# Normed attention with projections that come out transposed: head sums and roots through small tiles of the TensorE array

## The chip, the cores and the metric

The program runs on one NeuronCore of one Trainium2 chip, in one launch. The metric is the device time of that launch in microseconds (us); the median of three runs of the kernel before is 1232.67 us (1228.65 to 1232.94). The engines are called as in the profile: PE (TensorE products), PEld (its weight loads), DVE (VectorE), ACT (ScalarE), POOL (GpSimd).

## The reference, cut to what matters

Eight layers follow one another on 32 x 64 tokens of 128 numbers; each is `x = x + layer(layernorm(x))`. The change is in the third, an attention with 16 heads of 64 in which each head of the queries and of the keys is divided by its root mean square:

```python
def rms_norm(x, w):
    var = jnp.mean(jnp.square(x), axis=-1, keepdims=True)
    return x * jax.lax.rsqrt(var + EPS) * w
qh = (q @ Wq).reshape(b, l, HEADS, HEAD_DIM).transpose(0, 2, 1, 3)
kh = (kv @ Wk).reshape(b, s, HEADS, HEAD_DIM).transpose(0, 2, 1, 3)
vh = (kv @ Wv).reshape(b, s, HEADS, HEAD_DIM).transpose(0, 2, 1, 3)
qh = rms_norm(qh, q_norm_w)
kh = rms_norm(kh, k_norm_w)
scores = jnp.einsum('bhld,bhsd->bhls', qh, kh) * (1.0 / np.sqrt(HEAD_DIM))
scores = jnp.where(mask, scores, NEG_INF)
attn = jax.nn.softmax(scores, axis=-1)
o = jnp.einsum('bhls,bhsd->bhld', attn, vh)
return o.transpose(0, 2, 1, 3).reshape(b, l, HEADS * HEAD_DIM) @ Wo
```

Everything is float32. Each of the 32 sequences attends to 64 positions of its own context.

## The kernel before, in words

The 2048 tokens are 16 tiles of 128, worked on as 8 pairs of tiles (256 tokens, four sequences). Each layer is a stage that goes over the 8 pairs; each engine has its own instruction list, written by hand, and its order is the order in the code. Engines meet at semaphores. PE writes to a ring of six PSUM banks; a `Stage` holds a list of units such as `("s00", "v")`, one per filling of a bank, with the engine that empties it ("a" ACT, "v" DVE). Unit number j may fill its bank only when unit j - 6 has been emptied (`bank_free`). So the list sets both the order of fillings and who waits for whom. Two more banks lie outside the ring, one for the result (`ybank`) and one for turning the normed tokens (`xtbank`).

The normed attention (`att1`) is software-pipelined: an opening (`pro`) projects pair 0; the body (`body`, 7 times) works on the scores of pair p and on the projections of pair p + 1; a closing (`epi`) finishes pair 7. Per step of the body:

- PE: 64 products for the scores (line 1411); the queries and keys of the next pair as 8 products of 512 columns with the tokens as weights (1424); the result of the last pair (1481); 16 transposes of the probabilities (1358); 64 products for the mix (1467); the values (1440); 32 transposes of the scaled queries and keys (1452); the turn of the normed tokens (363).
- ACT: from each bank of projections a copy (1528) and a square (1529); the exponentials (1339); copies of the turned probabilities (1365); the reciprocal roots of the head sums as exp(-0.5 ln) (1553, 1555); copies of the mix (1560) and the values (1568); half of the turned queries and keys, scaled by the gain (1576).
- DVE: the softmax (mask and copy out of the bank 1315, maximum 1320, subtraction 1322, sum 1345, reciprocal 1347, product 1349); the sums of squares over each head (1591); the ending of the last pair (1864, 321 to 333: add to the stream, mean and variance, normed tokens); the division of tokens by their roots (1601); the other half of the turned queries and keys (1611).
- POOL: copies of the next inputs (2470, 2472) and the root of the variance for the ending (352).

With the tokens on the partitions, a head's sum of squares runs along a row, and the root is one number per partition and head. The scores need the head's 64 numbers on the partitions, so that the scaled tokens are transposed afterwards. The stage after next (`plain_attention`, twice) has the same softmax but no norms: its projections come out with the head's numbers on the partitions at once (1674).

## Time and profile before

| | us |
|---|---|
| median of 3 runs (lowest, highest) | 1232.67 (1228.65, 1232.94) |
| the profiled execution, its own time | 1232.76 |
| its span, first to last instruction | 1231.0 |
| PE, DVE, ACT, POOL busy | 1027.4, 855.5, 576.6, 222.0 |
[...]

Rows of a timeline read: start, duration, engine, line of the kernel, operation, what it writes and reads, how many in the group; in brackets the engine's idle time before and who ended it. On PE one product of float32 numbers is two instructions. The duration of a PE group includes the tail in which the last product leaves the array; the next group can start inside it. Busy shares are means over all stages; what matters here is one step of one stage.

### The profile page before, as it was taken

What the parts mean: (1) busy time and instruction counts of PE and PEld (TensorE: products, weight loads), DVE (VectorE), ACT (ScalarE), POOL (GpSimd) and SP (SyncE); (2) the same over time, 40 slices, a digit from 0 to 9 for tenths busy, and PEclk for the clock granted to TensorE, in tenths of its full rate; (3) what the DMA queues carried; (4) which work ended last, traced back from release to release, by engine and by line L of the source; (5) the groups of instructions that cost most, each with busy time, mean ns of one, the idle gap of its engine ahead of it and who ended that gap; (6) DMA issues with size and microseconds to landing.
All of it is one profiled execution on the core that took longest, in us unless ns stands there. A gap on an engine that the chain in (4) does not pass through costs nothing.

```text
span 1231.0 us, 32393 instructions
## 1 busy us (share of the span) xinstructions
PE 1027.4 (83%) x11974; PEld 816.6 (66%) x11974; DVE 855.5 (69%) x1903; ACT 576.6 (47%) x1119; POOL 222.0 (18%) x243
## 2 busy tenths in 40 slices
PE   5678999969888886899899999899998673798756
PEld 5357888746556566778678877678776562467546
DVE  5565677788999996555677676687675577667455
ACT  1223344556666663343555665465655220344343
POOL 3554122100111101331100000000000122343100
PEclk9877999989999998899999999999999885699778
DMA  9200000000000000000000000000000000000001
GB/s 369 95 2 1 0 0 0 0 2 2 0 0 0 0 0 2 2 1 1 2 2 0 0 0 2 2 1 0 0 0 2 1 0 0 1 1 0 1 0 34
DMA packets 5919, 16.13 MB, mean 13 GB/s; under 512 B 729, under 2 KB 4962, under 8 KB 5218
## 3 DMA queue, kind: packets, MB, share of 16 engines
q1 hardware_dynamic: 5858, 15.29, 3.2%
q8 instruction: 42, 0.69, 0.2%
q14 instruction: 19, 0.16, 0.0%
HBM read 14.24 MB, written 1.05 MB: 12 GB/s over the span
## 4 chain that ended last, share of the span: by engine, by line
PE 40%; issue 23%; DVE 18%; DVEq 11%; POOL 3%; ACT 2%; POOLq 2%; PEldq 1%; PEld 1%; ACTq 0%
PE banks L1674 7%; PE banks L1747 4%; PE banks L1719 3%; PE banks L1136 3%; PE banks L900 3%; PE banks L1707 3%; DVEq L1346 2%; PE banks L1358 2%; PE banks L1117 1%; PE banks L1735 1%; DVE small L1591 1%; DVE xn L333 1%; POOL small L832 1%; DVEq L1012 1%; DVE xr L1011 1%
## 5 line engine op out<-in xcount | busy, mean ns | idle before, releaser
L352 POOL TENSOR_TENSOR rstd<-var,nhalf 128x2 f32<-128x2 f32 x72 | 57.3, 796 | 483.0 <-DVE var L326 483.0
L1682 ACT ACTIVATE work<-banks 128x512 f32<-128x512 f32 x128 | 74.9, 600 | 70.2 <-PE banks L1674 70.2
L1339 ACT ACTIVATE work<-work 128x1024 f32<-128x1024 f32 x64 | 67.7, 1058 | 55.6 <-DVEq L1335 32.0
L374 ACT ACTIVATE xT_all<-banks 128x256 f32 (+1 forms) x72 | 28.3, 393 | 133.5 <-PE banks L363 133.0
L1674 PE MATMUL banks<-xT_all,weights 128*128 (+1 forms) x384 | 86.2, 380 | 2.3 <-ACT work L1792 1.8
L1358 PE MATMUL banks<-ident,work 128*128 128x128 f32 x512 | 71.0, 290 | 16.2 <-DVE work L1349 11.2
L1674 PEld LDWEIGHTS banks<-xT_all,weights 128*128 128x128 f32 x384 | 71.5, 190 | 13.7 <-ACT work L1792 2.6
L929 ACT ACTIVATE work<-banks,weights 128x256 f32<-128x256 f32 x128 | 53.6, 470 | 57.5 <-PE banks L890 56.5
L1358 PEld LDWEIGHTS banks<-ident,work 128*128 128x128 f32 x512 | 62.9, 150 | 23.3 <-DVE work L1349 13.3
L1826 DVE TENSOR_TENSOR work<-banks,neg_mask 128x512 f32<-128x512 f32 x64 | 40.7, 685 | 52.2 <-PE banks L1707 50.6
L363 PE MATMUL banks<-ident,xn 128*128 128x128 f32 x144 | 33.6, 320 | 43.7 <-DVE xn L333 38.4
L1747 PEld LDWEIGHTS banks<-weights,work 128*128 128x128 f32 x512 | 58.4, 191 | 14.9 <-ACT work L1792 14.8
L900 PE MATMUL banks<-weights,work 128*128 128x128 f32 x512 | 63.1, 276 | 3.7 <-DVE work L1003 3.4
L900 PEld LDWEIGHTS banks<-weights,work 128*128 128x128 f32 x512 | 60.9, 191 | 7.9 <-ACT work L929 6.9
L1747 PE MATMUL banks<-weights,work 128*128 128x128 f32 x512 | 61.0, 277 | 3.6 <-ACT work L1792 3.6
L890 PE MATMUL banks<-xs,weights 128*128 128x256 f32 x256 | 61.8, 390 | 0.0
L1349 DVE TENSOR_TENSOR work<-work,small 128x1024 f32<-128x1024 f32 x48 | 58.8, 1225 | 3.6
L1786 ACT ACTIVATE work<-banks 128x512 f32<-128x512 f32 x64 | 34.7, 595 | 55.7 <-PE banks L1735 55.5
L1345 DVE TENSOR_REDUCE small<-work 128x16 f32<-128x1024 f32 x48 | 58.2, 1212 | 0.0
L1365 ACT ACTIVATE work<-banks 128x512 f32<-128x512 f32 x96 | 52.1, 630 | 11.7 <-PE banks L1358 11.7
L1528 ACT ACTIVATE weights<-banks 128x512 f32<-128x512 f32 x64 | 41.1, 641 | 32.2 <-PE banks L1424 32.2
L363 PEld LDWEIGHTS banks<-ident,xn 128*128 128x128 f32 x144 | 18.2, 157 | 55.6 <-DVE xn L333 41.0
(311 smaller groups left out, 2413.3 us busy)
## 6 DMA issues: line engine op xcount, KB each, us to landing
weights<-wpack SPq DMA_DIRECT2D x1, 5381.5 KB, 32.1
weights<-wpack SPq DMA_DIRECT2D x1, 2060.0 KB, 13.2
weights<-wpack SPq DMA_DIRECT2D x1, 2049.0 KB, 17.5
weights<-wpack SPq DMA_DIRECT2D x1, 1160.5 KB, 19.8
x_all<-x_in SPq DMA_DIRECT2D x2, 512.0 KB, 4.8
ctxT_all<-ctxT_in SPq DMA_DIRECT2D x1, 1024.0 KB, 7.0
out<-x_all SPq DMA_DIRECT2D x8, 128.0 KB, 1.8
rows<-rows_in SPq DMA_DIRECT2D x1, 832.0 KB
```

The costliest lines, as they stand in the source:

```text
L352: g.tensor_tensor(rstd, var, nhalf[:, 0:2], ALU.pow).then_inc(rstd_ready, 1)
L890: ins = pe.matmul(bk[:, (c % 2) * PT:(c % 2 + 1) * PT], upw[:, c, :], xs[:], start=True, stop=True)
L900: ins = pe.matmul(bk[:, (2 * u + e % 2) * D:(2 * u + e % 2 + 1) * D], hT[:, e * chunks + c, u * P:(u + 1) * P], dnw[:, e * chunks + c, :], ...
L929: ins = act.activation(hT[:, c, :], bank(s.bank(name))[:, (c % 2) * PT:(c % 2 + 1) * PT], func, bias=w(pre + "_upb")[:, c:c + 1])
L1339: act.activation(sm[:, u, :], sm[:, u, :], ACT.Exp, scale=scale).then_inc(h["exp"].sem, 1)
L1345: v.reduce_sum(rs[:, u, :], every, AX)
L1349: v.tensor_tensor(every, every, rs[:, u, :, None].to_broadcast([P, 16, S]), ALU.mult) \
L1358: ins = pe.transpose(bank(s.bank(name))[:, c * P:(c + 1) * P], sm[:, u, 512 * half + c * P:512 * half + (c + 1) * P], ident[:])
L1365: act.activation(pT[:, u, 4 * half:4 * half + 4, :].rearrange("p c t -> p (c t)"), bank(s.bank(f"p{u}{half}")), ACT.Copy).then_inc(act_emp ...
L1674: ins = pe.matmul(bank(ring.bank(f"qk{c}"))[:, j * PT:(j + 1) * PT], wt[:, 2 * (c % 4) + j, :], cols(src, p), start=True, stop=True)
L1682: act.activation(dst.rearrange("p c t -> p (c t)"), bank(ring.bank(f"qk{c}")), ACT.Copy) \
L1747: ins = pe.matmul(ybank[:, u, :], oT[:, u, c, :], wo[:, c, :], start=(c == 0), stop=(c == 7))
```

## The change

The projections of queries and keys are now computed as in the plain attention: weights stationary, tokens moving, so that the heads' numbers come out on the partitions and nothing has to be transposed. A head's sum of squares then runs over partitions, and is formed by products: `head_sum` (128 x 32, ones in two columns) against the squares, on four column tiles (128 rows x 32 columns of the array each), that write to four strips of one bank. ACT makes the reciprocal roots of the bank (128 x 256). A second group of products spreads them over the partitions again, with the gains in the weights: each uses one row tile (32 rows x 128 columns) and writes one half bank. DVE multiplies the stored heads by these eight banks, in place. The squares of four of the eight banks go from ACT to POOL (`pooled`), except in the opening. The opening is moved to the end of the stage before (`tensor_head`, `scalar_head`, `vector_head`), and `make_gains`, a few small DVE operations, into its first step. POOL copies only the context.

The units of the ring, and the core of the new code:

```diff
-        att1 = pipelined(scores4, mixing8, [(f"tok{u}{c}", "a") for u in range(2) for c in range(4)],
-                         values4 + [(f"turn{u}{c}", "av"[c % 2]) for u in range(2) for c in range(4)])
+        scaling8 = [(f"bc{c}", "v") for c in range(8)]
+        att1 = stage([])
+        att1.pro = stage([("gains", "a")] + queries8 + [("sums", "a")] + scaling8 + values4, 1, shift=2)
+        att1.body = stage(scores4 + queries8 + [("sums", "a")] + turned4 + scaling8 + mixed4 + values4, PAIRS - 1)
+        att1.epi = stage(scores4 + turned4 + mixed4, 1)
...
+            pooled = (0, 2, 4, 6)
...
+            def make_gains(v):
+
+                v.wait_ge(weights_in[group], 16)
+                v.memset(head_sum, 0.0)
+                for k in range(2):
+                    v.tensor_scalar(gains[:, k, :], ident[:], w("a1_norm")[:, k:k + 1], None, ALU.mult)
+                v.drain()
+                for m in range(4):
+                    ins = v.tensor_copy(head_sum[:, m, :, 2 * m:2 * m + 2], parity[:, None, :].to_broadcast([P, 2, 2]))
+                ins.then_inc(gains_made, 1)
...
+            def sums(pe, ring, i, p):
+                settle(pe)
+                pe.wait_ge(*ring.emptied(i, "qk7"))
+                if ring is s.body and pooled:
+                    pe.wait_ge(*pool_squared.at(p - 1, 1))
+                settle(pe)
+                pe.wait_ge(*ring.bank_free(i, "sums"))
+                bk = bank(ring.bank("sums"))
+                for m in range(4):
+                    for j in range(4):
+                        ins = pe.matmul(bk[32 * j:32 * j + 32, 0:PT], head_sum[:, m, 0, :],
+                                        squares[j // 2][:, 4 * (j % 2) + m, :], start=(m == 0), stop=(m == 3),
+                                        tile_position=(0, 32 * j))
+                ins.then_inc(banks_filled, 1)
+
+            def roots_spread(pe, ring, i, p):
+                pe.wait_ge(*roots_made.at(p, 1))
+                for m in range(4):
+                    for j in range(4):
+                        name = f"bc{4 * (m // 2) + j}"
+                        if m % 2 == 0:
+                            settle(pe)
+                            pe.wait_ge(*ring.bank_free(i, name))
+                    for j in range(4):
+                        name = f"bc{4 * (m // 2) + j}"
+                        ins = pe.matmul(bank(ring.bank(name))[:, PT * (m % 2):PT * (m % 2) + PT],
+                                        gains_spread[32 * j:32 * j + 32, P * m:P * m + P],
+                                        head_roots[32 * j:32 * j + 32, :], start=True, stop=True,
+                                        tile_position=(32 * j, 0))
+                        if m % 2:
+                            ins.then_inc(banks_filled, 1)
...
+            def tensor_head(pe):
...
+                for k in range(2):
+                    for m in range(4):
+                        ins = pe.matmul(bank(s.pro.bank("gains"))[S * k:S * k + S, P * m:P * m + P],
+                                        head_sum[:, m, :, :].rearrange("p k r -> p (k r)"), gains[:, k, :],
+                                        start=True, stop=True)
...
+                def part(ring, i, p, last=True):
+                    if ring is s.body:
+                        pe.wait_ge(*ring.emptied_before(i, "bc7"))
+                        settle(pe)
+                    scores(ring, i, 0)
+                    scores(ring, i, 1)
+                    if ring is s.body:
+                        project(pe, ring, i, p + 1)
+                    if last:
+                        result([ring.emptied_before(i, f"o{u}1") for u in range(2)] if ring is s.body else None)
+                    if ring is s.body:
+                        sums(pe, ring, i, p + 1)
+                    probs_turned(pe, ring, i, p, 0, h["prob"])
+                    probs_turned(pe, ring, i, p, 1, h["prob"])
+                    if ring is s.body:
+                        roots_spread(pe, ring, i, p + 1)
+                        settle(pe)
+                        pe.wait_ge(*ring.emptied_before(i, "v3"))
+                    mix(ring, i, 0)
+                    mix(ring, i, 1)
+                    if ring is s.body:
+                        values(pe, ring, i, p + 1)
+                    turn_normed(pe, g_of(s, p))
...
+            def projected(act, ring, i, c):
+                act.wait_ge(banks_filled, ring.filled(i, f"qk{c}"))
+                k, a = c // 4, 2 * (c % 4)
+                bk = bank(ring.bank(f"qk{c}"))
+                ins = act.activation((kT if k else qT)[:, a:a + 2, :].rearrange("p c t -> p (c t)"), bk, ACT.Copy)
+                if ring is s.pro or c not in pooled:
+                    ins = act.activation(squares[k][:, a:a + 2, :].rearrange("p c t -> p (c t)"), bk, ACT.Square)
+                ins.then_inc(act_emptied, 1)
+
+            def head_roots_made(act, ring, i):
+                act.wait_ge(banks_filled, ring.filled(i, "sums"))
+                act.activation(head_roots, bank(ring.bank("sums"))[:, 0:PT], ACT.Ln, bias=eps[:, 0:1],
+                               scale=1.0 / 64).then_inc(act_emptied, 1)
+                act.drain()
+                act.activation(head_roots, head_roots, ACT.Exp, scale=-0.5).then_inc(roots_made.sem, 1)
...
+            def scaled(v, ring, i):
+                for k in range(8):
+                    v.wait_ge(banks_filled, ring.filled(i, f"bc{k}"))
+                    v.tensor_tensor(heads_of(k), bank(ring.bank(f"bc{k}")).rearrange("p (c t) -> p c t", t=PT),
+                                    heads_of(k), ALU.mult).then_inc(dve_emptied, 1)
...
+            def pool(g, p):
+
+                for c in pooled:
+                    k, a = c // 4, 2 * (c % 4)
+                    own = (kT if k else qT)[:, a:a + 2, :]
+                    g.wait_ge(*s.body.emptied(p, f"qk{c}"))
+                    ins = g.tensor_tensor(squares[k][:, a:a + 2, :], own, own, ALU.mult)
```

ACT's order in a step is: banks 0 and 1, first exponential, banks 2 to 5, second exponential, banks 6 and 7, roots, then as before.

The opening and the first step on PE, before (the names are those of the program's tensors; `banks` is PSUM, `work` holds queries, keys and probabilities, `xs` and `cs` are the pair's inputs; the 64x64 rows are scores, then mixes):

```order
L1424 MATMUL banks<-weights,xs 128x512 x2
L1424 MATMUL banks<-weights,cs 128x512 x2
L1440 MATMUL banks<-weights,cs 128x512 x4
L1452 MATMUL banks<-ident,weights 128x128 x32
L1411 MATMUL banks<-work 64x64 x64
L1424 MATMUL banks<-weights,xs 128x512 x2
L1424 MATMUL banks<-weights,cs 128x512 x2
L1358 MATMUL banks<-ident,work 128x128 x16
L1467 MATMUL banks<-work 64x64 x64
L1440 MATMUL banks<-weights,cs 128x512 x4
L1452 MATMUL banks<-ident,weights 128x128 x32
L363 MATMUL banks<-ident,xn 128x128 x2
```

The same place of PE, now (`free` with 32x256 is `head_sum` against the squares, `small,free` the roots against the gains):

```order
L1471 MATMUL banks<-work,free 64x128 x8
L1418 MATMUL banks<-xT_all,weights 128x256 x8
L1418 MATMUL banks<-ctxT_all,weights 128x256 x8
L1432 MATMUL banks<-weights,free 32x256 x16
L1447 MATMUL banks<-small,free 128x256 x16
L1460 MATMUL banks<-weights,cs 128x512 x4
L1493 MATMUL banks<-work 64x64 x64
L1352 MATMUL banks<-ident,work 128x128 x16
L1511 MATMUL banks<-work 64x64 x64
L357 MATMUL banks<-ident,xn 128x128 x2
```

The 32 transposes behind the values are gone. The sums stand behind the projections, ahead of the transposes of the probabilities, and the spread between those and the mix.

DVE in the first step behind the second maximum of the softmax, before:

```order
L1345 TENSOR_REDUCE small<-work 128x16
L1347 RECIPROCAL small<-small 128x16
L1349 TENSOR_TENSOR work<-work,small 128x1024
L1591 TENSOR_REDUCE small<-work 128x16 x4
L1594 TENSOR_SCALAR small<-small 128x64
L1601 TENSOR_TENSOR weights<-weights,small 128x1024 x4
L1611 TENSOR_SCALAR work<-banks,weights 128x4x128 x4
```

And now:

```order
L1339 TENSOR_REDUCE small<-work 128x16
L1341 RECIPROCAL small<-small 128x16
L1343 TENSOR_TENSOR work<-work,small 128x1024
L1620 TENSOR_TENSOR work<-banks,work 128x512 x8
```

Three groups behind the softmax have become one. In the later steps the ending of the last pair stands between 1343 and 1620; before, its first part stood ahead of 1601 and its second part, which needs POOL's root, behind it.

## Rows read from the trace of the kernel before

**Rows 1.** The page: span, then busy time (share) x instructions of an engine.
```profile
span 1231.0 us, 32393 instructions
...
PE 1027.4 (83%) x11974; PEld 816.6 (66%) x11974; DVE 855.5 (69%) x1903; ACT 576.6 (47%) x1119; POOL 222.0 (18%) x243
```

**Rows 2.** Timeline of PE in the stage: start, duration, what, [idle before].
```profile
258.52 2.23 PE L1411 MATMUL banks<-work 64*64 64x64 f32 x128 [1.34 <-DVE work L1611]
...
286.44 2.48 PE L1411 MATMUL banks<-work 64*64 64x64 f32 x128 [1.01 <-DVE work L1611]
...
315.93 2.53 PE L1411 MATMUL banks<-work 64*64 64x64 f32 x128 [1.28 <-DVE work L1611]
...
325.37 3.73 PE L1481 MATMUL banks<-weights,work 128*128 128x128 f32 x32
...
339.28 1.96 PE L1452 MATMUL banks<-ident,weights 128*128 128x128 f32 x16 [0.90 <-ACT work L1568]
...
462.92 2.23 PE L1411 MATMUL banks<-work 64*64 64x64 f32 x128 [1.24 <-DVE work L1611]
```

**Rows 3.** Stretches: length, PE, PEld, DVE, ACT, POOL busy (count), clock, DMA, GB/s.
```profile
315.90:345.40 29.50, 25.44 (x362) 17.75 (x363) 26.75 (x35) 19.54 (x37) 3.78 (x3) 1.00 0.00 0
638.20:659.90 21.70, 20.95 (x358) 17.27 (x348) 15.71 (x25) 13.22 (x23) 1.10 (x2) 1.00 0.00 0
```

**Rows 4.** Timeline of DVE in the third step.
```profile
317.24 1.29 DVE L1315 TENSOR_TENSOR work<-banks,neg_len 128x512 f32<-128x512 f32 x2 [1.76 <-PE banks L1411]
...
329.23 1.23 DVE L1349 TENSOR_TENSOR work<-work,small 128x1024 f32<-128x1024 f32 x1
330.37 4.59 DVE L1591 TENSOR_REDUCE small<-work 128x16 f32<-128x1024 f32 x4
...
336.79 5.03 DVE L1601 TENSOR_TENSOR weights<-weights,small 128x1024 f32<-128x1024 f32 x4
...
342.26 2.71 DVE L1611 TENSOR_SCALAR work<-banks,weights 128x512 f32<-128x512 f32 x4
```

**Rows 5.** Timeline of the plain attention, PE and the ending on DVE.
```profile
649.96 7.07 PE L1674 MATMUL banks<-xT_all,weights 128*128 x32
...
651.60 0.42 DVE L1891 TENSOR_TENSOR xr<-banks,tok_all 128x256 f32<-128x256 f32 x1
...
653.97 0.60 DVE L333 TENSOR_SCALAR xn<-xr,mv,rstd 128x128 f32<-128x128 f32 x2 [0.82 <-POOL rstd L352]
...
656.87 1.91 PE L1358 MATMUL banks<-ident,work 128*128 128x128 f32 x16
...
664.06 3.70 PE L1719 MATMUL banks<-weights,xs 128*128 128x512 f32 x8
```

**Rows 6.** Timeline of PE where small tiles stand now.
```profile
517.53 1.15 PE L1146 MATMUL banks<-free 32*128 32x256 f32 x16
...
1091.00 1.09 PE L2172 MATMUL banks<-weights,cs 128*64 128x128 f32 x16
```

**Rows 7.** Line 2172, its weight loads: ns minimum/median/maximum, first and last start.
```profile
L2172 PEld LDWEIGHTS banks<-weights,cs x128: 132/136/231, 1065.8 to 1157.3; 128*64 128x64 f32 x128
```

**Rows 8.** Timeline of ACT: first copy, last square of the opening; an exponential.
```profile
236.93 0.60 ACT L1528 ACTIVATE weights<-banks 128x512 f32<-128x512 f32 x1 [2.36 <-PE banks L1424]
...
244.09 0.78 ACT L1529 ACTIVATE work<-banks 128x512 f32<-128x512 f32 x1
...
321.17 1.06 ACT L1339 ACTIVATE work<-work 128x1024 f32<-128x1024 f32 x1 [0.53 <-DVE work L1322]
```

**Rows 9.** Groups of POOL by shape: count | busy us, mean ns | idle before.
```profile
L790 POOL TENSOR_TENSOR work<-xT_all,qmask 128x512 f32<-128x512 f32 x8 | 8.3, 1038 | 0.9 <-issue 0.8
...
L2470 POOL COPY xs<-xT_all 128x256 f32<-128x256 f32 x10 | 4.0, 396 | 16.0 <-PEq L906 7.9 <-PEq L1722 4.2 <-PEq L1443 3.9
```

**Rows 10.** Timeline of POOL in the third step.
```profile
339.35 1.39 POOL L2472 COPY cs<-ctxT_all 128x256 f32 x1
```

**Rows 11.** A stretch of the opening, columns as in rows 3.
```profile
250.00:252.00 2.00, 0.61 (x3) 0.61 (x4) 2.00 (x3) 0.88 (x2) 0.00 (x0) 0.50 0.00 0
```

More of the change, by code:

```diff
@@ L1625, in step @@
                         end[0](v, s, p - 1)
-                    if normed and nxt:
-                        divide(p + 1)
-                    if this and last:
                         end[1](v, s, p - 1)
-                    if normed and nxt:
-                        turned(ring, i)
-                step(s.pro, 0, -1, False, True)
-                step(s.body, 0, 0, True, True, last=False)
-                with v.Fori(1, PAIRS - 1) as p:
-                    step(s.body, p, p, True, True)
-                step(s.epi, 0, PAIRS - 1, True, False)
+                    if ring is s.body:
+                        scaled(v, ring, i)
```

374 lines of the change are left out of this document (149 added, 225 removed).

## Prediction

> **What bounds the kernel now.** First the page's head: the span is 1231.0 us in the profiled execution, PE is busy for 83% and DVE for 69% of it [rows 1]. These are means over eight stages, so the stage of the change is read by itself. The next view is the timeline of PE. The scores of a pair open each step of the normed attention, at 258.52 (first step), 286.44 (second), 315.93 (third), and at 462.92 for the closing one [rows 2]. The six steps between 286.44 and 462.92 take 176.48 us, 29.4 each; the first takes 27.9.
>
> The view by stretches of one such step shows DVE busy for 26.75 of 29.5 us at a full clock, PE for 25.44. One step of the following plain attention, which has the same softmax and the same products but no norms of heads, takes 21.7 us with PE at 20.95 and DVE at 15.71 [rows 3]. So the norms cost 7.7 us a step and turn a PE-bound step into a DVE-bound one. The timeline of DVE shows it: between 317.24 and the end of L1611 at 344.97 it has no idle stretch; its one wait is 1.76 us for the first scores, and the scores had waited for DVE's last L1611 [rows 2, 4]. DVE sets the end, PE stands at its back only from the last scaled bank to the first score.
>
> **What the change takes off DVE, per step.** Four sums of squares (L1591), 4.59 us; four divisions (L1601), 5.03; four scaled copies out of the transposes (L1611), 2.71; together 12.3 us with no cover, as DVE is the bound [rows 4]. It adds eight products bank x work of 128x512. Their form is that of L1315, 1.29 us for two in a row [rows 4], so 8 x 0.65 = 5.2. DVE falls from 26.7 to about 19.6 us of work in a step.
>
> **What it does to PE, per step.** Removed: the 32 transposes of scaled queries and keys (two groups of 16, L1452, 1.96 us with its tail [rows 2]), about 3.6. Unchanged in columns: the 8 projections, formerly tokens as weights with 512 columns, now 16 products of 256 columns; 32 instructions of just this kind last 7.07 in the plain attention [rows 5]. Added: 16 products for the sums and 16 for the spread, each two instructions of 256 columns. On the whole array such an instruction costs 7.07/32 = 0.22, which would be 7.1 for each of the two groups. On tiles it is less. Rows of 32 x 128 stand in the trace: 16 instructions of 256 columns in 1.15 us, a tail of about 0.2 included, against 16 x 0.22 = 3.5: nearly four run at once. Columns of 128 x 32 do not; the nearest are 128 x 64, where 16 instructions of 128 columns last 1.09, tail of about 0.25 included, against 16 x 0.11 = 1.8 on the whole array, so two column tiles run beside each other [rows 6]. Bounds for the sums are thus 1.75 (four at once) and 7.1 (in a line), with 3.6 for two at once. I take 1.85: four row tiles reach nearly four and two column tiles nearly two. The spread is 2 x 1.15.
>
> [...]
>
> **The new step, laid out.** Zero is the start of the scores.
> PE does scores until 2.5, projections until 9.5, the result product of the last pair (L1481, 3.73 with tail [rows 2]) until 13.1. The sums wait there for the copies and squares of all eight banks. ScalarE starts one such operation each 0.48 (sixteen between 236.93 and 244.09 [rows 8]) and has 12 of them and two exponentials of 1.06 [rows 8] between: the last square ends near 12.0. GpSimd's four squares cost 1.04 each by L790 [rows 9]; the last can start at about 11.1 and end at 12.2 to 13.1. So the sums run 13.1 to 14.95, and the 16 transposes of probabilities (1.91 [rows 5]) to 16.8; DVE's probabilities were ready at 14.5, as now (329.23 + 1.23 - 315.93 [rows 2, 4]). ScalarE's logarithm and exponential of 128x256, about 0.4 each, fall under the transposes. Then it copies the turned probabilities, and the fourth bank of the spread is that of the second copy, so the spread starts at about 17.1. Its first half fills four banks at 18.2.
> DVE has meanwhile done the ending of the last pair: 14.5 plus 2.97 (from 651.60 to 654.57 in the plain attention, the root by GpSimd included [rows 5]) is 17.5. That root was hidden behind the divisions; it is bare now, but it ends before the first spread bank. DVE scales two banks until 19.6. Only then may PE fill the second half, because its last two banks are those of the first two; that half is full at 20.75. The first mix needs the bank of the fourth scaling (20.9) and the second mix that of the sixth (22.2): mixes end at 23.4, values (3.70 with tail [rows 5]) at 27.0, the turn of the normed tokens at 27.3. I take 27.5 for the step.
> So PE becomes the bound, with some 2.5 us of waits for DVE left in it between 16.8 and 20.9. The gain is 29.4 - 27.5 = 1.9, though DVE loses 7: the rest is DVE idling. Behind each added wait on PE stand the mixes and values, and nobody waits for those but ScalarE.
>
> **The other terms.** Six such steps: -11.5. First step: no result product, no ending; the sums wait for the squares and the spread for the roots, 27.5 to 28.5 against 27.9: +0.1. Opening: eight products for the gains come first (about 1.8 on PE, which can start some 0.8 sooner), so the same sixteen copies and squares of ScalarE begin 1.0 later than at 236.93 and the last ends at 245.9 [rows 8]. Then sums (247.8), roots (248.9), first half (250.1), two scalings (251.4), second half (252.5), and DVE's last scaling at 255.5; the last copy of the values ends at about 257, against scores at 258.52. [...] I take -0.5, within -2 and +1.5. Seven small DVE operations that make the gains, about 1.3 us in all, lie in the stage before, where DVE waits for PE in each pair: +0.3, at most 1.3. One copy of 128x256 per pair goes from GpSimd: nothing. The stages behind are untouched.
> Sum: -11.5 + 0.1 - 0.5 + 0.3 = -11.6. The profiled execution took 1232.76, 1.76 more than its span and 0.1 above the median of 1232.67, so the forecast is 1232.8 - 11.6 = 1221.2. A measurement of this kernel tells 0.5%, 6.2 us, from no change.
>
> **Rivals.**
> 1. Column tiles run only two at a time. The sums then take 3.6, all of it on PE's path, as roots and spread follow: +1.75 in each of eight places, +14, 1235. For it: no row shows more than two. Against it: the row tiles show that four streams can be fed. 9%.
> 2. GpSimd and DVE stop each other. A copy of 128x256 on GpSimd takes 0.396 alone and 1.39 while DVE runs L1601 [rows 9, 10]. If each of the four squares holds up one of DVE's four operations with two inputs in SBUF (L1322 and L1349, twice) for its whole 1.04, DVE's probabilities come 4.1 later. PE needs the second at about 15.9 and they are ready at 14.5, so 1.4 is absorbed and 2.7 not: seven steps give +19, 1240.5, slower than before. It decides from a mean delay above 0.9 per square. Against it: ScalarE spaces the squares out, and two of them start while DVE reads a bank or reduces. 7%. [...]
> 3. The same, mild: the last square ends 1 us after PE is ready for the sums. +1 in seven steps: 1228. 8%.
> 4. [...] 3%.
> 5. PE loses less at the banks than laid out (the second half of the spread starts closer behind the first scaling, the opening keeps its clock): steps of 26.7 and -2 in the opening give 1215. It is the low end of the forecast's own case.
>
> **How the numbers follow.** Forecast with rival 5: 73%, all of it faster by over 0.5%. Rivals 1 and 3: 17%, within 0.5%. Rivals 2 and 4: 10%, slower. The range runs from 1213 (steps of 26.5, a good opening) to 1234 (nearly the whole of rival 1), and leaves out rivals 2 and 4 and a few per cent below.
>
> **What the new profile would show.** Steps of 27.5 from scores to scores. DVE idle for about 8 of them, above all before the eight products on banks. [...] The two halves of the spread 2.5 us apart, the second released by DVE. GpSimd's squares near 1.04, and L1322 and L1349 still at 1.23; longer ones mean rival 2. PE waiting at the sums for GpSimd means rival 3. I am wrong at the root if the step is again DVE's, or if PE's wait stands anywhere but between the transposes and the mixes.

## The result, and the profile after

| | median us (lowest to highest, runs) | ratio to before, 95% interval |
|---|---|---|
| before | 1232.16 (1228.65 to 1232.94, 4) | |
| after | 1241.56 (1239.11 to 1243.94, 4) | 1.0072 [1.0047, 1.0097] |

The changed kernel is slower by 0.7%, where 1221.2 us was forecast. The profiled execution took 1239.11 us, the shortest of the four. The head of its page, as in [rows 1]:

```profile
span 1237.4 us, 33362 instructions
...
PE 1027.7 (83%) x12374; PEld 830.1 (67%) x12374; DVE 800.9 (65%) x1871; ACT 549.0 (44%) x1060; POOL 245.8 (20%) x263
```

DVE lost 54.6 us of work, as meant; PE kept its 1027. The stretch of one looped step, from scores to scores (columns as in [rows 3]):

```profile
407.45:436.67 29.22, 25.59 (x410) 19.76 (x410) 19.78 (x30) 15.72 (x29) 7.21 (x6) 1.00 0.00 0
```

DVE falls from 26.75 us to 19.78, the 19.6 of the forecast, and yet the step is 29.22 us long where it was 29.49. PE is busy for 25.59 of it, so 3.6 us of waits must stand on PE. Its timeline in this step shows where:

```profile
407.45 1.21 PE L1493 MATMUL banks<-work 64*64 64x64 f32 x64 [1.08 <-issue]
...
417.10 3.73 PE L1525 MATMUL banks<-weights,work 128*128 128x128 f32 x32
420.77 1.94 PE L1432 MATMUL banks<-weights,free 128*32 128x256 f32 x32
422.64 1.97 PE L1352 MATMUL banks<-ident,work 128*128 128x128 f32 x16
424.78 1.15 PE L1447 MATMUL banks<-small,free 32*128 32x256 f32 x16 [0.17 <-ACT work L1359]
427.28 1.15 PE L1447 MATMUL banks<-small,free 32*128 32x256 f32 x16 [1.36 <-DVE work L1620]
428.57 1.16 PE L1511 MATMUL banks<-work 64*64 64x64 f32 x64
430.04 1.16 PE L1511 MATMUL banks<-work 64*64 64x64 f32 x64 [0.31 <-DVE work L1620]
431.13 3.70 PE L1460 MATMUL banks<-weights,cs 128*128 128x512 f32 x8
435.19 0.41 PE L357 MATMUL banks<-ident,xn 128*128 128x128 f32 x2 [0.35 <-issue]
436.67 1.21 PE L1493 MATMUL banks<-work 64*64 64x64 f32 x64 [1.08 <-issue]
```

Counted from the scores: sums (L1432) at 13.3, transposes (L1352) 15.2, spread (L1447) 17.3 and 19.8, mixes (L1511) 21.1 and 22.6, values (L1460) 23.7 to 27.4. The forecast had 13.1, 14.95, 17.1, 19.65, 20.9, 22.2, 23.4 to 27.0. So 0.4 us had come together by the end of the values. The rest is in the tail: 0.35 us ahead of the turn (L357), and 1.08 between it and the next scores, both "issue", that is, nobody had to be waited for.

Not all looped steps are like this one. From scores to scores, the six intervals behind the first step are 30.71, four of 29.22 to 29.24, and 28.47 to the closing step, 176.1 us in all where before had 176.48.

The waits of PE over the six such steps, summed (us in total, times, longest):

```profile
PE banks L1447 <- DVE work L1620: 8.2, 6, 1.4
PE banks L1493 <- issue: 7.7, 12, 1.1
PE banks L357 <- issue: 2.1, 6, 0.4
PE banks L1511 <- DVE work L1620: 1.9, 6, 0.3
```

Before, the scores waited for DVE 8.7 us in all over the same stretch, in seven waits of up to 1.3 [rows 2]; now they and the turn wait 9.8 us for the issue of instructions.

The opening, PE after; before, the scores stood at 258.52 [rows 2]:

```profile
240.00 3.62 PE L1418 MATMUL banks<-ctxT_all,weights 128*128 128x256 f32 x16
245.70 1.94 PE L1432 MATMUL banks<-weights,free 128*32 128x256 f32 x32 [2.08 <-ACT weights L1563]
249.43 1.15 PE L1447 MATMUL banks<-small,free 32*128 32x256 f32 x16 [1.79 <-ACT small L1571]
251.91 2.09 PE L1447 MATMUL banks<-small,free 32*128 32x256 f32 x16 [1.33 <-DVE work L1620]
253.93 5.77 PE L1460 MATMUL banks<-weights,cs 128*128 128x512 f32 x8
260.99 1.21 PE L1493 MATMUL banks<-work 64*64 64x64 f32 x64 [1.29 <-ACT work L1576]
```

After three waits (5.2 us idle of 8.3) the second half of the spread takes 2.09 us where the first took 1.15, and the values 5.77 where a looped step has 3.70. The stretch of that second half says why: the granted clock was 0.50 of the full one; over the values it was 0.64 in the mean.

```profile
251.90:254.00 2.10, 2.09 (x17) 1.29 (x17) 1.15 (x2) 0.00 (x0) 0.00 (x0) 0.50 0.00 0
253.93:259.70 5.77, 5.77 (x12) 2.23 (x8) 2.48 (x4) 1.79 (x3) 0.00 (x0) 0.64 0.00 0
```

The kernel before has a stretch at 0.50 in its opening too, from 250 to 252 [rows 11], where PE comes back from 5.04 us of waiting:

```profile
251.39 5.78 PE L1452 MATMUL banks<-ident,weights 128*128 128x128 f32 x32 [5.04 <-DVE weights L1601]
```

The third loss lies where nothing was changed. At the border of the two plain attentions the groups of 64x64 products break off and go on later:

```profile
774.73 1.95 PE L1748 MATMUL banks<-work 64*64 64x64 f32 x104
778.29 0.58 PE L1748 MATMUL banks<-work 64*64 64x64 f32 x24 [1.61 <-issue]
...
803.15 2.50 PE L1720 MATMUL banks<-work 64*64 64x64 f32 x123 [1.36 <-ACT work L1359]
806.64 0.34 PE L1720 MATMUL banks<-work 64*64 64x64 f32 x5 [0.98 <-issue]
```

The same group in the profile of before is whole:

```profile
770.13 2.38 PE L1735 MATMUL banks<-work 64*64 64x64 f32 x128
```

A mark by which kernels can be compared place by place is the start of the turn of the normed tokens on PE (L363, L357). The table gives it for before, and for the others the difference to it (negative: earlier). It is one execution of each, and ahead of the stage, where nearly the same code has run, they already differ by over 3 us; so differences between rows say more than a row.

| place | before | after | a_nodrain | e_after_split | f_open_split | c_both | e_both_split |
|---|---|---|---|---|---|---|---|
| last turn ahead of the stage | 232.25 | -0.28 | +3.08 | +2.16 | +1.62 | +1.68 | +1.79 |
| first scores | 258.52 | +2.47 | +4.30 | +6.79 | -0.16 | -0.11 | +0.01 |
| last turn before the closing step | 461.30 | +3.11 | -2.65 | +6.32 | -8.20 | -14.95 | -15.96 |
| border of the plain attentions, start | 769.71 | +4.60 | +0.17 | +4.68 | -8.86 | -10.35 | -15.14 |
| the same, end | 819.93 | +7.78 | +2.79 | +4.87 | -9.23 | -8.02 | -15.76 |
| last turn | 1174.33 | +7.34 | +5.86 | +6.45 | -11.87 | -9.55 | -17.71 |
| looped step (the fifth interval), us | 29.49 | 29.22 | 27.55 | 29.04 | 27.52 | 26.47 | 26.47 |

The miss can be laid out for the profiled executions. That of after is 6.4 us longer than that of before (1239.11 against 1232.76), where 11.6 less was forecast: a miss of 18.0 us. The six intervals hold 11.1 of them (176.1 against 6 x 27.5), the opening 3.3 (+2.75 against -0.5), and what lies behind the closing scores 4.2 (from +2.2 there to +6.4 at the end of the span); the stages ahead give 0.6 back.

### The profile page after: what moved, and what is told of

It reads as the page before. It is cut to its first block, busy times and chain, and to the rows that moved or that the text cites. A ratio compares the mean times of both kernels' runs of the same rounds, so it can differ in the third digit from the quotient of the medians.

```text
span 1237.4 us, 33362 instructions
## 1 busy us (share of the span) xinstructions
PE 1027.7 (83%) x12374; PEld 830.1 (67%) x12374; DVE 800.9 (65%) x1871; ACT 549.0 (44%) x1060; POOL 245.8 (20%) x263
## 4 chain that ended last, share of the span: by engine, by line
PE 49%; issue 21%; DVE 12%; DVEq 8%; POOL 4%; ACT 3%; POOLq 1%; PEldq 1%; PEld 0%; ACTq 0%
PE banks L1687 7%; PE banks L1760 4%; PE banks L1732 4%; PE banks L1418 3%; PE banks L1131 3%; PE banks L894 3%; PE banks L1720 3%; PE banks L1352 2%; PE banks L1460 2%; PE banks L1748 2%; PE banks L1525 1%; PE banks L1112 1%; PE banks L1447 1%; POOL small L826 1%; PE banks L1493 1%
## 5 line engine op out<-in xcount | busy, mean ns | idle before, releaser
L346 POOL TENSOR_TENSOR rstd<-var,nhalf 128x2 f32<-128x2 f32 x72 | 51.4, 714 | 359.5 <-DVE var L320 359.5
L1352 PE MATMUL banks<-ident,work 128*128 128x128 f32 x512 | 68.9, 287 | 9.6 <-DVE work L1343 8.0
L1352 PEld LDWEIGHTS banks<-ident,work 128*128 128x128 f32 x512 | 61.7, 148 | 16.9 <-DVE work L1343 9.8
L357 PE MATMUL banks<-ident,xn 128*128 128x128 f32 x144 | 32.5, 312 | 44.6 <-DVE xn L327 35.5
L357 PEld LDWEIGHTS banks<-ident,xn 128*128 128x128 f32 x144 | 17.3, 152 | 61.3 <-DVE xn L327 36.9
L1309 DVE TENSOR_TENSOR work<-banks,neg_len 128x512 f32<-128x512 f32 x32 | 20.6, 684 | 53.6 <-PE banks L1493 53.6
## 6 DMA issues: line engine op xcount, KB each, us to landing
weights<-wpack SPq DMA_DIRECT2D x1, 2049.0 KB, 17.1
```

The costliest lines, as they stand in the source:

```text
L346: g.tensor_tensor(rstd, var, nhalf[:, 0:2], ALU.pow).then_inc(rstd_ready, 1)
L1352: ins = pe.transpose(bank(s.bank(name))[:, c * P:(c + 1) * P], sm[:, u, 512 * half + c * P:512 * half + (c + 1) * P], ident[:])
```

## The experiments

The letter of a label is its group. Before was measured again beside each group; its medians are 1233.05 (a, with b_shift128), 1231.93 (c, with b_shift16), 1232.30 (d), 1233.05 (e) and 1232.39 (f). Ratios are to the executions of before in the same group.

**The tail of the step.** Theory: `values` ends in a drain of PE that marks the inputs as used. The loop's branch stands behind it, with only the turn between. While PE's queue stands in the drain it gets nothing ready ahead, so branch and first scores are issued bare. Rival: the branch alone, or the wait for ScalarE's store of the turned tokens. The trace shows when the drain is over, by the copy on GpSimd that it releases:

```profile
435.06 0.40 POOL L2485 COPY cs<-ctxT_all 128x256 f32 x1 [10.48 <-PEq L1463]
```

The queue's own instructions are in the trace too (PEldq). The drain, in all eight places, and the branch of this step in after:

```profile
L1463 PEldq DRAIN  x8: 2940/2942/4387, 255.4 to 461.2; - x8
L1395 PEldq COMPARE_BRANCH  x1: 208/208/208, 435.3 to 435.3; - x1
```

and the branch of the same step in a_nodrain, described next:

```profile
L1395 PEldq COMPARE_BRANCH  x1: 208/208/208, 428.7 to 428.7; - x1
```

In after the drain stands from 431.95 to 434.89, and between its end and the scores at 436.67 lie eleven small instructions of the queue: four semaphore increments, a wait that is met, five register operations and the branch of 0.21 us. The branch itself is thus the smaller part of the gap. In a_nodrain these instructions pass while the values are still running (427.56 to 431.27).

a_nodrain takes the drain away; ScalarE marks the inputs once it has copied the values:

```diff
-                pe.drain().then_inc(inputs_used, 1)          # values (PE)
+                act.sem_inc(inputs_used, 1)                  # values_taken (ACT), behind the four copies
```

> The changed kernel, but in the normed attention PE has no drain behind the value products: the mark that the pair's inputs have been read comes from ScalarE, which has waited for the last value bank anyway. Theory 1 (the drain stands just ahead of the turn and of the loop's jump, so PE's sequencer can't run ahead and the array is empty while turn, jump and waits are issued): the step of 29.2 us falls to about 27.8, the turn follows the values without the 0.35 us gap, the scores follow the turn within 0.3 to 0.5 us in place of 1.5; 7 steps give -9, about 1232. Rival (the jump itself or the fetch of the loop's code costs the 1.1 us): only 0.35 a step goes, -2.5, about 1239.

Measured 1234.26 us (1230.87 to 1238.99), 1.0008 [0.9990, 1.0026]. The step is 27.55 us, the forecast's 27.5 (27.8 was expected), and its tail has closed:

```profile
427.56 3.71 PE L1460 MATMUL banks<-weights,cs 128*128 128x512 f32 x8
431.10 0.38 PE L357 MATMUL banks<-ident,xn 128*128 128x128 f32 x2
431.41 1.21 PE L1492 MATMUL banks<-work 64*64 64x64 f32 x64
```

a_unroll keeps the drain and takes the loop away on PE alone:

```diff
+                        if eng is nc.tensor:
+                            for p in range(1, PAIRS - 1):
+                                part(ring, p, p)
+                            continue
                         with eng.Fori(1, PAIRS - 1) as p:
```

> The changed kernel with PE's six looped steps of the normed attention written out, so that PE has no jump there; the drain stays. Theory 1 (the drain keeps the sequencer from running ahead; the jump of 0.2 us and its refill are only a part of what it exposes): about 0.5 to 0.8 a step goes, the 0.35 us gap before the turn stays; -3 to -5 from the steps, and up to +3 from more code to fetch. Rival (the jump is the cost): the gap between turn and scores falls from 1.1 idle to 0.1, 1.0 a step, and a variant without the drain would win only 0.35 a step.

Measured 1233.82, 1.0009 [0.9986, 1.0032], nearly 3 us below what the theory gave (1236.5 to 1241.5). The gap before the turn stays (0.25), and that before the scores falls to 0.17, as the rival had it:

```profile
427.13 3.71 PE L1464 MATMUL banks<-weights,cs 128*128 128x512 f32 x8
431.09 0.41 PE L357 MATMUL banks<-ident,xn 128*128 128x128 f32 x2 [0.25 <-issue]
431.68 2.38 PE L1497 MATMUL banks<-work 64*64 64x64 f32 x128 [0.17 <-ACT work L1580]
```

This step is 27.87 us long and one other 27.91; the remaining three of the five are 29.0 to 29.3, with gaps of 1.1 to 1.5 us of issue at other places (see the place of the code below). Written out, the steps have lost the branch and the register operations with it; the wait and four increments are left between drain and scores.

So it takes both: a drain, and a branch with its register operations behind it, with next to nothing between. Taking away either closes the tail. f_before_nodrain is the control, the kernel before with the same edit.

> The kernel before with the same edit as the first experiment: no drain behind the values of its normed attention; ScalarE marks the inputs used. There 16 + 16 transposes stand between the drain and the loop's end, and the next scores wait 1.28 us for DVE. If a drain costs only where nothing is queued between it and the branch, the step stays 29.47 us and the time 1232 within 1.5. Rival, a drain costs by itself wherever it stands: the step falls by 0.5 us or more, 3 us and more in all.

Measured 1231.30, 0.9996 [0.9980, 1.0012]; the step is 29.47, as good as the 29.49 of before. There 32 transposes stand between drain and branch. But the first of them wait 0.90 us for ScalarE and the next scores 1.28 for DVE, with and without the drain; so the control shows that the drain was free there, and not which of the two hid it, the transposes or these waits.

**The squares.** a_allact puts all of them on ScalarE: `pooled = ()`.

> The changed kernel with all eight squares on ScalarE and none on GpSimd. In the looped steps the last square then ends about 1.4 us later than now (3 more of 0.48 ahead of it), which is about when PE reaches the sums: step 29.2 to 29.7. The first step, where PE waits 3.3 us for GpSimd's last square, loses nothing or gains 0.5 to 1. If GpSimd's squares (1.5 on average beside DVE) and DVE's slowed subtractions (1.42 for 1.22) were what ate the gain, this would be faster by 1 to 3 us a step; I expect within 3 us of the changed kernel, 1239 to 1244.

Measured 1248.02, 1.0123 [1.0093, 1.0152], 0.5% above after and 4 us above what was expected. The first step did not gain: its sums wait 3.95 us for ScalarE's last square, where they waited 3.32 for GpSimd's, and then take 3.37 us. In a looped step (29.62) PE now waits at the sums:

```profile
426.17 1.95 PE L1432 MATMUL banks<-weights,free 128*32 128x256 f32 x32 [0.52 <-ACT weights L1563]
```

GpSimd is the right place for half of them, although rival 2 is real in small: in a_nodrain the squares take 1557 ns in the median against 1039 at least, and in after one DVE operation, L1316, takes up to 1619 against 1224. In the looped steps all of that is absorbed.

**The opening.** c_open issues two of the four values ahead of the sums and two behind them (on top of a_nodrain):

```diff
-        att1.pro = stage([("gains", "a")] + queries8 + [("sums", "a")] + scaling8 + values4, 1, shift=2)
+        att1.pro = stage([("gains", "a")] + queries8 + values4[:2] + [("sums", "a")] + values4[2:] + scaling8, 1, shift=2)
```

> The kernel after without the drain behind its values (as in the first experiment), and in the opening alone two of the four values stand ahead of the sums and two between the sums and the spread, so that TensorE has 7.5 us less of idle time in a row there. If the opening lost its 3 us because TensorE waited for ScalarE and DVE with the values still unissued (clock halved at the second spread and the values), the first scores start 3 to 5 us earlier than in the run without the drain (there 262.82 us with a start that is 3.3 us late; so about 258.5), the spread and values show their full-clock durations (1.15 and 3.7 us), and the time falls to about 1230. Rival: the opening is bound by the eight scalings on DVE and the clock falls all the same; then the scores start within 1 us of where they did.

Measured 1229.54, 0.9993 [0.9972, 1.0014], which is not told from a_nodrain by the medians. In the traces the scores start at 258.23 against 262.82 (3.0 us sooner, counted from the last turn ahead of the stage), and the spread keeps its 1.15. But the low clock was only put off: PE now waits 3.32 us for DVE's scalings ahead of the scores, and these take 3.75 us in place of 2.38, at a granted clock of 0.50. At the next turn 2.3 of the 3.0 are left. The theory held for the place and its clock, and gave too much for the price.

**The order in the step.** c_order moves the two mixes between the halves of the spread (on top of a_nodrain), where PE waited 1.36 us for banks; c_both is both edits.

```diff
-... + turned4 + scaling8 + mixed4 + values4, PAIRS - 1)
+... + turned4 + scaling8[:4] + mixed4 + scaling8[4:] + values4, PAIRS - 1)
```

> The kernel after without the drain, and in the looped step the two mixes stand between the first and the second half of the spread, where TensorE waited 1.36 us for DVE to empty banks and 0.31 us before the second mix. If the step without the drain is bound by TensorE's work and these two waits, it falls from 27.55 to 25.9-26.3 us (TensorE is busy 25.6 of it), six steps save 8 to 9 us, and the time is about 1226. Rival: DVE then ends its scalings later, and the next scores wait for them by as much as was saved: the step stays above 27 us.

> Both edits on the kernel without the drain: values among the sums in the opening, mixes between the halves of the spread in the looped step. If the two gains are of different places they add: first scores 3 to 5 us earlier and a step of 25.9-26.3 us, together 11 to 14 us on 1234.3, so about 1221. Rival: the displacement of TensorE's code downstream takes a part back (up to 5 us by the kernels so far): 1222 to 1230.

Measured 1225.12, 0.9944 [0.9918, 0.9969], and 1221.24, 0.9933 [0.9909, 0.9956]. The step falls to 26.47 us; 0.54 is left ahead of the second half:

```profile
410.96 1.15 PE L1449 MATMUL banks<-small,free 32*128 32x256 f32 x16 [0.17 <-ACT work L1361]
412.04 1.16 PE L1513 MATMUL banks<-work 64*64 64x64 f32 x64
413.56 1.16 PE L1513 MATMUL banks<-work 64*64 64x64 f32 x64 [0.36 <-DVE work L1626]
415.26 1.15 PE L1449 MATMUL banks<-small,free 32*128 32x256 f32 x16 [0.54 <-issue]
```

Both times are as expected (1226 and 1221), but the expectation for the step (25.9 to 26.3) had no term for that 0.54. c_both is 14.95 us ahead of before at the end of the stage, but only 8.02 behind the border of the plain attentions. That loss is the next question.

**The place of the code.** The built program of before has 11005 instructions for PE; that of after has 401 more, c_both 398, and a_unroll 4274 more than after. How code is brought in stands in the pages of before, after and a_unroll (packets, MB):

```profile
q8 instruction: 42, 0.69, 0.2%
q8 instruction: 44, 0.72, 0.2%
q8 instruction: 61, 1.00, 0.4%
```

a_unroll is longer on PE alone, and q8 alone has grown in it (q14, the other queue of this kind, has 19 packets in all three), so q8 is PE's instruction queue. 0.69 MB in 42 packets are 16 KB a packet, and 0.69 MB over 11005 instructions are 63 bytes each; a_unroll's 17 packets more, over its 4274 instructions, give 65. I take 64 bytes, 256 instructions a packet, as an estimate from these (11005/42 is 262, 15680/61 is 257). Theory: where 64x64 products are issued at one per 19 ns (128 instructions in 2.38 us), what they cost depends on how the code lies in these packets. b_shift128 and b_shift16 put 128 and 16 semaphore increments ahead of PE's first work in the kernel before (`for _ in range(n): settle(pe)`).

> The kernel before with 128 idle semaphore increments ahead of PE's first wait, where PE waits for the first inputs anyway: nothing computed or ordered differently, only every later PE instruction lies 128 places further on. If about 4 us of the changed kernel's loss come from where its code lies (gaps of 1.0 to 1.6 us inside groups of small products, at the first pass over a piece of code, and clock phases that follow), this moves the time by 1 to 4 us in either direction and shows such gaps in other places. Rival: the place of the code is of no account, the time is that of the kernel before within 1 us.

> The kernel before with 16 semaphore increments ahead of TensorE's first work and nothing else. In the run with 128 of them 6 of the 10 us lay before the first turn. If these are the increments' own time, 16 cost under 1 us there; what stays behind that is the place of TensorE's code in memory. If the place of the code by itself matters for the stages that are fetched during 64x64 products, this kernel is 0 to 4 us off the one before after subtracting the start; if it does not, it is within 1 us.

Measured 1242.96, 1.0078 [1.0051, 1.0105], and 1233.37, 1.0015 [0.9998, 1.0032]. The first is far outside the 1 to 4 us that were expected. With 128, 6 us were lost before the first turn, so the increments themselves were suspect. d_before_place128 has them in a wait of 5.85 us in the first stage; d_after_place111 and d_both_place114 fill the displacement of after and c_both up to 512, two packets.

> The kernel before with 128 increments in the idle stretch at 33.7 us in place of ahead of all work. If 6 of the 10 us of the earlier run with 128 were the increments' own time, and the rest the place of the code (half a packet on), turn 4 stays within 1 us of before, and the same later losses show: about 1.7 us before the attention stage, 2.6 at turns 42 to 44; time 1235-1237. Rival, all of it the increments' own time: 1232.

> The kernel after with 111 semaphore increments on TensorE's queue while it waits 5.85 us for DVE in the first stage (33.7 to 39.5 us), nothing else. TensorE's program of after is 401 instructions of 64 bytes longer than that of before; with these 111 it is 512 longer, twice the 256 instructions (16 KB) that one packet of its instruction queue carries. If the losses behind the changed stage (turn 29 to 44: 2.9 to 7.8 us later than before) and the 'issue' gaps within the 64x64 products are the place of the code in those packets, the losses behind turn 28 vanish to within 1 us and the kernel comes to 1236-1238. Rival: they come from the time at which things meet; then after stays at 1241.5.

> The kernel with both edits (values among the sums in the opening, mixes between the halves of the spread, no drain) and 114 increments in the same idle stretch, so that its code behind the stage lies 512 instructions on from where it lay in before. If the place of the code costs what is lost there (against before, -14.9 us at turn 25 becomes -8.0 at turn 44 and -9.5 at the end), the gain stays at 14-15 us to turn 50 and the time is about 1216. Rival: 1221 as without them.

Measured 1249.87 (1.0140), 1249.08 (1.0125) and 1228.55 (0.9965 [0.9947, 0.9983]): all three lie 11 to 13 us above what was expected. An increment was taken to cost 47 ns, 6 us over 128; it costs three times that, as the first product behind the 128 shows, released by nobody:

```profile
51.61 1.97 PE L602 MATMUL banks<-work 128*64 128x256 f32 x8 [18.80 <-issue]
```

18.80/128 is 0.147 us each; in b_shift128 most of it had lain under PE's first wait of 14 us. Past that point the marks spoke for the theory: between 769.71 and 819.93 d_after_place111 lost 0.1 us (after 3.2) and d_both_place114 won 0.3 (c_both lost 2.3). So the padding was split so that it hides: 79 or 80 increments ahead of the first work, the rest in the wait.

> The kernel after, 111 increments in two places at which TensorE idles longer than they take (0.147 us each in the run before): 79 ahead of all work (idle 13.7 us), 32 in the wait of 5.85 us at 33.7 us. Its code behind the stage lies 512 instructions on from that of before. If the place of the code is what costs behind the stage, the turns to 18 are as in after, turns 42 to 44 lose nothing (3.2 us in after), and the time is 1236 to 1239 in place of 1241.5. Rival: no effect of the place: 1241.5.

> The kernel with both edits and no drain, 80 increments ahead of all work and 34 in the wait at 33.7 us; code behind the stage 512 instructions on from before. By the place of the code: turn 25 14.9 us ahead of before as without them, turn 44 still 13 to 15 us ahead (8.0 without), time 1215 to 1218 in place of 1221.2. Rival: 1221.

> The kernel before with 80 increments ahead of all work and 34 in the wait at 33.7 us: the same padding, but its code lies 114 instructions on, under half a packet. By the place of the code it loses where the others stop losing: about 2 us at turns 42 to 44 and 1233 to 1236 in all. If the padding itself costs or gains time, turn 4 shows it. Rival: as before, 1232.3.

Measured 1239.37, 1.0046 [1.0029, 1.0062]; 1214.16 (1212.40 to 1220.12), 0.9858 [0.9835, 0.9880]; 1234.03, 1.0011 [0.9996, 1.0025]. The first is just above the range that the theory gave (1236 to 1239), the second just below its own (1215 to 1218), with 15.76 us of lead where c_both had 8.02; the third is inside. In e_after_split the broken group is whole again:

```profile
774.81 2.38 PE L1750 MATMUL banks<-work 64*64 64x64 f32 x128
```

What each kernel loses against before over that border, by how many instructions its code lies further on, modulo 256:

| displacement mod 256 | loss between 769.71 and 819.93, us |
|---|---|
| 0 (six kernels, 512 on) | -0.6 to +0.2 |
| 253 (f_before_nodrain), 16, 67 | -0.2, +0.4, -0.6 |
| 114, 128 (two) | +1.2, +2.1 and +2.7 |
| 142 (four), 145 (two) | +2.3 to +6.7, +3.2 and +4.5 |

The control e_before_split has the loss in its trace (1.2) and no difference in its median that can be told. So the place of the code is shown as a cause where 64x64 products stand in a row. Three pairs of kernels have intervals that do not meet: c_both with e_both_split, a_nodrain with f_nodrain_split, c_open with f_open_split. After and e_after_split differ by 2 to 3 us with intervals that do meet.

It costs in the changed stage too. The second step, the first pass over the loop's code, is 1.1 to 2.4 us longer than the later ones in all six looped kernels made from after whose code was not padded (30.71 for 29.23 in after, 29.97 for 27.55 in a_nodrain), and no longer in the six that were.

What comes in ahead of the gaps stands in the DMA rows of the trace. A packet of PE's instruction queue starts at 775.71 in after, here in a stretch of 0.2 us (16 KB in 0.2 us are the 82 GB/s of the last column):

```profile
775.60:775.80 0.20, 0.20 (x20) 0.15 (x11) 0.00 (x0) 0.00 (x0) 0.00 (x0) 1.00 0.40 82
```

The products break off at 776.68 and go on at 778.29, 2.58 us behind the packet's start. The other five gaps of 0.9 us or more inside groups of 64x64 products in after (they end at 292.55, 756.27, 806.64, 811.06 and 941.45) end 2.4 to 2.8 us behind the start of a packet too. A whole group of 128 instructions on PE and as many weight loads is one packet by the estimate above, and it is gone in 2.38 us. So these gaps look like waits for code. That the place decides whether the next packet is asked for early enough is my guess and not shown; why 114 to 145 are bad and 16 or 67 not was not worked out.

**Do the causes add up?** f_nodrain_split and f_open_split are a_nodrain and c_open with the same padding to 512; the second is the kernel of the forecast, with its step in its own order.

> The kernel after without the drain behind its values, with 80 and 34 increments in TensorE's two idle stretches (code behind the stage 512 instructions on from before). If drain, opening and place of the code are the whole miss, what is left of it is the opening's 3 us (5 where the clock falls further) and 1 to 2 us at turns 4 to 11: 1225 to 1228, in place of 1234.3 with the code in its unpadded place. Rival: the padded and the unpadded kernel are equal, 1234.

> The same with the opening's values among the sums; the looped step is the one of the kernel after, in its order, without the drain. It is the kernel that the forecast of 1221.2 spoke of: step 27.5, opening 0 to 2 us faster than before. If the three causes are all, 1220 to 1223. Rival: something else of the change costs too, 1226 or more.

Measured 1227.76, 0.9966 [0.9950, 0.9982], as expected, and 1224.03, 0.9941 [0.9919, 0.9963], 1 us above what was expected. In time (a difference of ratios times 1232.7): place of the code 3.2 us (after to e_after_split), drain 9.9 (to f_nodrain_split), opening 3.1 (to f_open_split). With the intervals these are good to 3 or 4 us each, so that of the three only the drain's is clear of the noise; their sum, 16.1, is firmer. The unpadded pair (after, a_nodrain) gives 7.9 for the drain. The traces are narrower here: the six intervals fall by 7.5 us without it in both pairs (176.1 to 168.6, and 173.6 to 166.1). All of that is in five of them. The interval to the closing step keeps its 28.5: with the drain there is no branch back to expose (0.32 us of issue), without it the scores wait 0.89 us for ScalarE's copies of the values.

## Why the prediction was wrong, point by point

- **The step that failed**: "values (3.70 with tail [rows 5]) at 27.0, the turn of the normed tokens at 27.3. I take 27.5 for the step." The steps were laid out by what PE waits for and how long it works, and not by when its queue can issue. The drain in `values` was in the old code too, so it counted as no change. But the change took away the 32 transposes behind it and the wait for DVE ahead of the scores, and the queue's own small instructions came to lie bare between values and scores. Measured: 1.5 to 1.7 us in a looped step, 7.5 us over the six intervals by the traces, 7.9 and 9.9 by the medians of two pairs. Without the drain the step is 27.55. Two more terms were missing in the same sum: the first pass over the loop's code (2.4 us in a_nodrain, nothing in f_nodrain_split) and the interval to the closing step (28.5, 1.0 above the 27.5).
- **The opening** was to be -0.5 within -2 and +1.5, and came out at +2.75 over the marks (from -0.28 to +2.47). Its layout ends at about 257 against scores at 258.52, which is 1.5 sooner; no run shows the 1.0 between that and the -0.5 as a term. What they show in its place is work at a low clock: 0.94 us in the second half of the spread (2.09 for 1.15, at 0.50) and 2.07 in the values (5.77 for 3.70, at 0.64). Moving the values won 2.3 us of it back in the traces (up to the next turn); the clock then fell in the first scores.
- **"The stages behind are untouched."** Their code was, its place was not: 3.2 us in this kernel (after to e_after_split, not clear of the noise), 5 to 9 in the three others that were padded to 512 in both places. In those the loop's first pass has a part of it.
- **The gains**: +0.3 forecast, +0.8 in the trace (the marks go from -1.03 to -0.24 between the first two turns of the stage before, where `make_gains` stands, and stay there to its end).
- **First step**: 28.05 us against 27.92, +0.1 as forecast, with 3.32 us of waiting for GpSimd's last square in it (3.95 for ScalarE's where it makes them all).
- **What was right**: DVE at 19.78 (19.6); column tiles four at a time, 1.94 us for 32 instructions (1.85), which rules out rival 1 (3.6), and also weight loads that stand in line, the number 4 of the chances (32 of 110 ns are 3.5); the spread in halves 2.5 us apart, released by DVE; PE as the bound. Rival 2 is there in kind and absorbed (its sum is 1240.1, not 1240.5); rival 3 holds in the first step only. Rival 5 was right that time could still be had at the banks, but not by itself: only with the mixes moved there is the step 26.47.
- **Still open**: f_open_split stands 4 us above the forecast (0.9941 against 0.9907). 0.5 of it are the gains; 0.9 is the interval to the closing step (28.43 for 27.5); its first step, with scores and sums at the low clock (3.75 and 3.52 for 2.38 and 1.95), is 29.92 us long against 28.05 in after, which is 1.9 more. The rest is within the intervals. Also open is a loss of 1.8 to 2.0 us in the stage behind, which seven kernels have (after, a_nodrain, a_unroll, c_both and three that were padded to 512) and the others not (0.3 at most, e_after_split and f_open_split among them), so it is not the place of the code alone.

## What to carry to other kernels

When you take work off an engine, look at what stands behind a drain in its queue. Here branch, register operations and increments cost nothing where other work covered them (the values in a_nodrain) or where PE waited anyway (before and f_before_nodrain, 29.49 and 29.47 us a step), and 1.08 us a step where they came to lie bare; laying out a step by waits and durations alone did not show that. Here the engine that reads the results could mark the inputs as used, and the drain on PE was not needed. Where a kernel has long runs of very short products, try a few displacements of the code before judging a change of less than 0.5%: here it was worth 3 to 9 us by itself. The version with all four (no drain, values among the sums, mixes between the halves, code 512 instructions on) beats both kernels, at 1214.16 us (0.9858 of before).

## What the runs showed of the hardware

- A weight load of column tiles does not stand in line: 32 loads of 110 ns (3.5 us) and 32 instructions of 380 ns each went by in 1.94 us. On the whole array 32 instructions of 256 columns take 7.07 [rows 5], 3.6 times as long, so nearly four run at a time:

```profile
L1432 PEld LDWEIGHTS banks<-weights,free x256: 106/110/113, 245.7 to 451.3; 128*32 128x32 f32 x128
L1432 PE MATMUL banks<-weights,free x256: 377/380/403, 245.7 to 451.6; 128*32 128x256 f32 x128
```

  Loads in line would have made it at least 3.5 us. The tiles of 128 x 64 in the kernel before are alike: 16 loads of 136 ns in the median [rows 7], 2.2 us in line, went by in 1.09 [rows 6].

- A semaphore increment by itself on PE's queue took 0.147 us where nothing covered it (18.80 us for 128).
- A drain followed by the end of the loop cost 1.4 us a pass in bare issue (0.35 and 1.08), of which the branch is 0.21. With the drain alone 0.25 lay bare, with the branch alone nothing.
- Inside groups of 64x64 products, PE stopped for 0.9 to 1.6 us and went on 2.4 to 2.8 us behind the start of a 16 KB packet of its instruction queue (all six such gaps in after).
- PE's granted clock was 0.50 behind the three waits of the opening in after (251.90 to 254.00), and in c_open behind one of 3.32 us (258.20 to 262.00); in both the work right behind them paid (2.09 us for 1.15, and 3.75 for 2.38).
